# Edge passes of a graph attention kernel in another layout: groups of ten with a carry column, 79 tiles, one addition over 1024 columns, the next weights split first, the join prepared in the drain

## What is computed

```python
loops = arange(N); src, dst = concat([src, loops]), concat([dst, loops])
xl = (x @ Wl + bl).reshape(N, H, C)
xr = (x @ Wr + br).reshape(N, H, C)
e = leaky_relu(xl[src] + xr[dst], 0.2)
logits = einsum('ehc,hc->eh', e, att)
m = segment_max(logits, dst); p = exp(logits - m[dst])
alpha = p / segment_sum(p, dst)[dst]
out = segment_sum(xl[src] * alpha[..., None], dst) + bias
# x = x + layer1(elu(layer0(layernorm(x)))); x = x + ffn(layernorm(x))
```

## Time and profile before

| | |
|---|---|
| runs, median (range) | 3017.18 us (3014.49 to 3019.19) |
| profiled execution | 3014.56 us, its span 3012.7 us |
| busy in the span | PE 87%, DVE 83%, ACT 50%, POOL 41% |
| edge pass 0 / 1, first addition to the next stage's first DMA | 559.0 to 1043.5 us / 1597.2 to 2081.3 us |
| VectorE busy, 640 to 960 / 1680 to 2000 us | 308.15 / 310.85 of 320 us |
| tiles started in each of these | 58 / 58 |
| granted TensorE clock there | 0.95 / 0.94 |
| DMA share there | 0.86 / 0.86 |

### The profile page before, as it was taken

One profiled execution on the slowest core, in us unless ns is written; L12 is line 12 of the kernel. 1 busy time (PEld: TensorE's weight loads), 2 busy tenths in 40 slices (PEclk: granted clock), 3 DMA queues, 4 the chain that ended last, 5 costly groups with the idle time before them and its releaser, 6 DMA issues. The chain is left out here.

```text
span 3012.7 us, 40248 instructions
## 1 busy us (share of the span) xinstructions
PE 2627.5 (87%) x11205; PEld 1801.0 (60%) x11205; DVE 2505.0 (83%) x5771; ACT 1503.3 (50%) x3651; POOL 1236.6 (41%) x1138
## 2 busy tenths in 40 slices
PE   6999999788888099999989888861899999969997
PEld 5777777333333078888864333330788888746665
DVE  7999998699999467777757999994988888379997
ACT  4545555155555333333323555553777788525554
POOL 0012220577776133333317777752333333014443
PEclk8999999899999599999999999985899999989998
DMA  9999999588887588888856888876999999469999
GB/s 326 340 308 319 320 323 342 179 235 243 231 238 211 142 272 279 269 265 266 263 197 204 243 239 237 237 186 202 385 357 352 347 349 344 140 183 250 249 250 160
DMA packets 321178, 789.66 MB, mean 262 GB/s; under 512 B 53838, under 2 KB 54384, under 8 KB 310746
## 3 DMA queue, kind: packets, MB, share of 16 engines
q1 hardware_dynamic: 220440, 540.20, 51.2%
q0 software_dynamic: 98064, 243.10, 33.3%
q10 hardware_dynamic: 2452, 3.79, 0.4%
HBM read 469.66 MB, written 329.28 MB: 265 GB/s over the span
## 5 line engine op out<-in xcount | busy, mean ns | idle before, releaser
L882 PE MATMUL bank<-wr,nT_e 128*128 128x512 f32 x1280 | 610.6, 622 | 0.5 <-DVE z_e L735 0.5
L1039 PE MATMUL bank<-whi,t_hi 128*128 128x512 f32 x1256 | 524.0, 417 | 23.7 <-DVE t_lo L406 23.7
L1041 PE MATMUL bank<-whi,t_lo 128*128 128x512 f32 x1256 | 498.1, 397 | 0.0
L1040 PE MATMUL bank<-wlo,t_hi 128*128 128x512 f32 x1256 | 497.7, 396 | 0.0
L882 PEld LDWEIGHTS bank<-wr,nT_e 128*128 128x128 f32 x1280 | 244.3, 201 | 253.1 <-issue 252.4
L906 POOL DMA_INDIRECT vin<-touched,node_slot x157 | 173.5, 1105 | 333.2 <-DMA vin<-rows 329.8
L906 POOL DMA_INDIRECT g_vin<-touched,node_slot x157 | 176.9, 1127 | 323.2 <-DMA g_xin<-in_x 289.8
L676 ACT COPY nT_e<-bank 128x512 f32<-128x512 f32 x160 | 93.6, 585 | 409.3 <-PE bank L885 354.9
L1039 PEld LDWEIGHTS bank<-whi,t_hi 128*128 128x128 f32 x1256 | 237.2, 189 | 73.7 <-issue 17.2
L1041 PEld LDWEIGHTS bank<-whi,t_lo 128*128 128x128 f32 x1256 | 237.2, 189 | 58.8
L655 POOL TENSOR_TENSOR z_e<-z_e,v_att 128x512 f32<-128x512 f32 x160 | 204.8, 1280 | 158.6 <-DVE z_e L740 157.8
(11 more groups left out here) (247 smaller groups left out, 6001.5 us busy)
## 6 DMA issues: line engine op xcount, KB each, us to landing
rows<-t_row SPq DMA_DIRECT2D x312, 512.0 KB, 4.4
w_e<-w_e POOLq DMA_DIRECT2D x80, 512.0 KB, 4.7
touched<-acc_e SPq DMA_DIRECT2D x160, 256.0 KB, 4.3
xin<-in_x SPq DMA_DIRECT2D x156, 256.0 KB, 4.7
xTin<-in_xT SPq DMA_DIRECT2D x156, 256.0 KB
vin<-rows SPq DMA_DIRECT2D x156, 256.0 KB, 4.0
g_vin<-rows SPq DMA_DIRECT2D x156, 256.0 KB
g_xin<-in_x SPq DMA_DIRECT2D x156, 256.0 KB
```

The costliest lines, as they stand in the source:

```text
L882: pe.matmul(psR[b][:, :], nT[:, b, cc, :], wr[:, cc, :], start=(cc == 0), stop=False)
L1039: pe.matmul(ps, hi[:, cc, :], whi[:, cc, :], start=(cc == 0), stop=False)
L1040: pe.matmul(ps, hi[:, cc, :], wlo[:, cc, :], start=False, stop=False)
L1041: last = pe.matmul(ps, lo[:, cc, :], whi[:, cc, :], start=False, stop=(cc == KC - 1))
```

## The change

- G is 10 instead of 5, and the last groups are of five and four tiles (`LAST`, `group_sizes`): nine groups for T = 79 tiles.
- The logits, maxima and sums of a group lie in one row with a carry column in front of each head's columns (`lg`, `top`, `total`; width H x (n + 1)). What comes over from the group before stands in the carry column, so that the factor needs no instructions of its own; `same_w` and `gap_w` replace `same4`, `gap4` and `gap4_back`.
- `vs` and `nv` become one `ring` of R = 18 places with three rows of 512; `pair_sums` is one addition over 1024 columns, xr broadcast. GpSimd now multiplies the first half of `z`, VectorE the second.
- GpSimd gathers LEAD = 6 ahead instead of 7. Weighing follows `weigh_at`: 11 steps behind in groups of ten, and for the last 30 tiles (`CATCH`) two tiles a step once their group is ready; adding follows one step and accumulating three steps behind it.
- The split of the next weights stands at the start of a pass. `raw`, `brow`, `others`, `share`, `weigh_s`, `share_T` and `picked` lie in places of `w1`, `w2`, `z` and `nT`.
- The trailing values are stored as soon as the last shares are there; `picked` and the arithmetic of the join stand ahead of the last accumulations.
- Every Block has `no_gpsimd_drain=True`.

The core of the diff:

```diff
-G = 5
-R = 14
+G = 10
+LAST = (5, 4)
+CATCH = 30
+LEAD = 6
+R = 18
+OWN, SRC = 0, 1
...
-    with nc.Block() as block:
+    with nc.Block(no_gpsimd_drain=True) as block:
...
-    T = -(-(e_tiles) // G) * G
+    T = e_tiles
+    W = T + len(group_sizes(T))
...
+    weigh_at = []
+    for t in range(T):
+        i = group_of[t]
+        ready = first[i] + sizes[i] + 1
+        weigh_at.append(max(ready, weigh_at[-1] + (0 if t % 2 and t > T - CATCH else 1)) if t else ready)
+    steps = weigh_at[-1] + 5
+
+    def due(k, at, late):
+        return [t for t in range(T) if at[t] + late == k]
...
+            for t in range(T):
+                if t == late[0]:
+                    sp.wait_ge(s["trail_set"], 2)
+                    sp.dma_start(trails[:, :], trail[:, :, :].rearrange("p a h -> p (a h)")).then_inc(s["trail_stored"], 16)
+                if t == late[1]:
+                    sp.wait_ge(s["trail_stored"], 16)
+                    sp.dma_start(others.rearrange("p q a h -> p (q a h)"),
+                                 bcast(trails[:, :].rearrange("q a -> (q a)"))).then_inc(s["others_loaded"], 16)
+                store(t)
...
-            pipeline(T + G + 2, [(lambda t: product_own(t) if t < T else None, 1),
-                                 (lambda t: add_own(t - G - 2) if t > G + 1 else None, 0),
-                                 (lambda t: gather(t) if t < T else None, 7)])
+            for k in range(-LEAD, steps):
+                if 0 <= k + 1 < T:
+                    product_own(k + 1)
+                for t in due(k, weigh_at, 1):
+                    add_own(t)
+                if 0 <= k + LEAD < T:
+                    gather(k + LEAD)
...
+            act.wait_ge(s["w_loaded"], 16)
+            act.copy(whi[:, :, :], raw).then_inc(s["w_high"], 1)
...
+            for k in range(-4, steps):
+                if 0 <= k + 4 < T:
+                    copy_transposed(k + 4)
+                for t in due(k, weigh_at, 0):
+                    weigh(t)
+                if 0 <= k < T:
+                    exps(k)
...
-                dve.tensor_tensor(z[:, b, 0, :], psR[t % 2][:, :], vs[:, u, :], ALU.add)
-                dve.tensor_tensor(z[:, b, 1, :], psR[t % 2][:, :], nv[:, u, 1, :], ALU.add).then_inc(s["z"], 1)
+                dve.tensor_tensor(z[:, b, :, :], psR[t % 2][:, :].unsqueeze(1).to_broadcast([P, 2, D]), ring[:, u, 1:3, :],
+                                  ALU.add).then_inc(s["z"], 1)
...
+                if i:
+                    dve.tensor_scalar(l[:, SRC, :, 0], columns(top, i - 1)[:, :, sizes[i - 1]], gap[:, at:at + 1], None, ALU.add)
+                link(dve.tensor_tensor(l[:, OWN, :, 1:], l[:, OWN, :, 1:], start_gap[:, at:at + n].unsqueeze(1).to_broadcast([P, H, n]),
                                        ALU.add))
+                link(dve.tensor_tensor(m, lg[:, OWN, a:b], lg[:, SRC, a:b], ALU.max))
+                link(dve.tensor_tensor_scan(m, gap_w[:, a:b], m, -BIG, ALU.add, ALU.max))
+                link(dve.tensor_tensor_scan(back(top, a, b), back(gap_w, a + 1, b + 1), m[:, ::-1], -BIG, ALU.add, ALU.max))
+                dve.tensor_tensor(lg[:, :, a:b], lg[:, :, a:b], top[:, a:b].unsqueeze(1).to_broadcast([P, 2, b - a]),
+                                  ALU.subtract).then_inc(s["bottom"], 1)
...
+                    link(dve.tensor_tensor(carry, carry, columns(total, i - 1)[:, :, sizes[i - 1]], ALU.mult))
+                link(dve.tensor_tensor(q, lg[:, OWN, a:b], lg[:, SRC, a:b], ALU.add))
+                link(dve.tensor_tensor_scan(total[:, a:b], same_w[:, a:b], q, 0.0, ALU.mult, ALU.add))
+                link(dve.tensor_tensor_scan(v[:, ::-1], back(gap_w, a + 1, b + 1), back(total, a, b), -BIG, ALU.add, ALU.max))
+                link(dve.reciprocal(v, v))
+                dve.tensor_tensor(lg[:, :, a:b], lg[:, :, a:b], v.unsqueeze(1).to_broadcast([P, 2, b - a]),
+                                  ALU.mult).then_inc(s["shares"], 1)
...
+            for k in range(-3, T):
+                for step, ahead in ((leaky, 2), (logits, 1), (pair_sums, 3), (product, 2), (peaks, 1)):
+                    if 0 <= k + ahead < T:
+                        step(k + ahead)
+                for t in due(k, weigh_at, 3):
+                    accumulate(t)
+                if k >= 0:
+                    sums_up(k)
+                if k == T - 1:
+                    dve.wait_ge(s["shares"], NC)
+                    dve.tensor_copy(trail[:, 0, :], columns(top, NC - 1)[:, :, sizes[-1]]).then_inc(s["trail_set"], 1)
+                    dve.tensor_copy(trail[:, 1, :], columns(total, NC - 1)[:, :, sizes[-1]]).then_inc(s["trail_set"], 1)
...
+def group_sizes(T):
+
+    sizes = []
+    while sum(sizes) < T - sum(LAST):
+        sizes.append(min(G, T - sum(LAST) - sum(sizes)))
+    return sizes + list(LAST)
```

More of the change, by code:

```diff
@@ L33 @@
 DR = 5
-SR = 4
 MR = 8
@@ L569, in edge_pass, with span, columns, columns2 @@
     places = touched[:, :].rearrange("(p t) d -> p t d", p=P)
-    N, NC = g["N"], T // G
     following = "Wl1" if layer == 0 else "gfc1T"
+    sizes = group_sizes(T)
+    first = [sum(sizes[:i]) for i in range(len(sizes))]
+    group_of = [i for i, n in enumerate(sizes) for _ in range(n)]
+    NC, W = len(sizes), T + len(sizes)
+    top_size = max(sizes)
+    def span(i):
+        a = H * (first[i] + i)
+        return a, a + H * (sizes[i] + 1)
+    def columns(buf, i):
+        a, b = span(i)
+        return heads(buf[:, a:b])
+    def columns2(buf, i):
+        a, b = span(i)
+        return buf[:, :, a:b].rearrange("p a (h n) -> p a h n", h=H)
+    def back(buf, a, b):
+        return buf[:, a:b][:, ::-1]
+    def share_of(buf, side, t, h):
+        i = group_of[t]
+        q = span(i)[0] + h * (sizes[i] + 1) + 1 + t - first[i]
+        return buf[:, side, q:q + 1]
+    def is_last(t):
+        return t == T - 1 or group_of[t + 1] != group_of[t]
+    weigh_at = []
+    for t in range(T):
+        i = group_of[t]
+        ready = first[i] + sizes[i] + 1
[3 more added lines that the diff above has]
+        return [t for t in range(T) if at[t] + late == k]
     with ExitStack() as c:
@@ L610, in edge_pass @@
             g["gathered_before"][t % R] += 32
-        block = c.enter_context(nc.Block())
+        block = c.enter_context(nc.Block(no_gpsimd_drain=True))
+        late = [t for t in range(T) if weigh_at[t] + 3 >= T]
         @block.sync
@@ L752, in logits @@
                                   ALU.add).then_inc(s["logit"], 1)
             def peaks(t):
-                i, last = divmod(t, G)
-                if last != G - 1:
+                if not is_last(t):
                     return
-                b, at = i % 2, i * G
-                l, m, e = lg[:, b, :, :, :], peak[:, b, :, :], ex[:, b, :]
-                factor = e[:, 2 * H * G:]
+                i = group_of[t]
+                at, n = first[i], sizes[i]
+                a, b = span(i)
@@ new lines, in _ @@
+            for i, n in enumerate(sizes):
+                dve.tensor_copy(picked[:, 0, :, first[i]:first[i] + n], columns(top, i)[:, :, 1:])
+                last = dve.tensor_copy(picked[:, 1, :, first[i]:first[i] + n], columns(total, i)[:, :, 1:])
+            link(last)
+            link(dve.tensor_tensor(picked.rearrange("p a h t -> p (a h) t"), picked.rearrange("p a h t -> p (a h) t"),
+                                   first_end[:, :].unsqueeze(1).to_broadcast([P, 2 * H, T]), ALU.mult))
@@ L839, in _ @@
+            link(dve.tensor_reduce(picked2[:, :, :], picked, AX.X, ALU.add))
+            mine = picked2
+            for k in range(T, steps - 2):
+                for t in due(k, weigh_at, 3):
+                    accumulate(t)
             dve.wait_ge(s["others_loaded"], 16)
[L840 removed]
+            link(dve.tensor_tensor(share, others[:, :, 0, :].rearrange("p q h -> p h q"),
                                    g["joins"][:, :].unsqueeze(1).to_broadcast([P, H, P]), ALU.add))
[L842 removed]
+            link(dve.tensor_reduce(best[:, :], share, AX.X, ALU.max))
```

202 lines of the change are left out of this document (73 added, 129 removed).

## The result

The changed kernel takes 3168.97 us (median of four, 3163.68 to 3178.37) against 3017.87 (3014.49 to 3019.19) beside it: ratio 1.0506, interval 1.0475 to 1.0537. It is slower, as forecast, but by 151 us instead of 20, outside the range. The profiled execution took 3174.08, its span 3172.4, where the forecast's sum had 3034.6. Medians are of all executions of a kernel; the one exception is e12, where an execution of 4848.36 us at a granted clock of 0.75 instead of 0.94 is left out.

What follows compares the result with a forecast made beforehand. VectorE bound the kernel at 5.40 us a tile, gather waits just under it. Two passes at +16 (start and steady part) and -4 (tail), and -4.2 for the last drain, gave +20: 3037 us (3034.6 profiled), range 2990 to 3075.

Steps and rivals of the forecast that it cites:

- tail: From a pass's last addition to the next stage: 55.5 us instead of 59.4, -4 us a pass.
- the price of the round: Chain of leaky, gather, transposes, root product and addition advances three tiles instead of four: 17.2 us, 5.73 a tile.
- issue to transposes: From GpSimd's issue of the second gather to TensorE's transposes: 5.74 us, or 5.16 on a lighter load.
- transposes to the addition: From TensorE's transposes through the root product to VectorE's addition: 4.63 us at the high clock.
- addition to leaky: On VectorE, from the addition to the next leaky: 2.40 us, with the 0.06 saved taken off.
- the merging: On VectorE, two additions over 512 columns become one over 1024: 0.06 us a tile saved.
- the drains: no_gpsimd_drain removes GpSimd's drain, 4.6 us at each edge pass's end and 4.2 at the kernel's end.
- the weight split: At the start of a pass: costs nothing, or up to 2 us if weights land after the first transposes.
- a shorter round: Rival, chance 0.20: the round is shorter than rows with waits say, 5.5 us a tile, 2995 us.
- a lead that does not matter: Rival, chance 0.08: VectorE's work alone counts, 5.1 us a tile from the twentieth on, 2931 us.
- The loss of the high clock: Rival, chance 0.12: TensorE's root products at half clock in half of the tiles, +0.3 us a tile, 3075 us.
- the longer tail: Rival, chance 0.11: last group's weighings stand ahead of its exponentials and the drain's wait turns up elsewhere, 3055 us.

Runs made afterwards that it cites:

- e12: e4 with the catch-up only for the last 12 tiles (CATCH = 12 instead of 30): 2958.06 us, ratio 0.9801.
- e1: The kernel before with one edit, GpSimd gathering 6 ahead instead of 7: 3160.93 us, ratio 1.0475.
- e2: The changed kernel with TensorE's transposes 5 ahead instead of 6, so a round advances four tiles: 2989.12 us, ratio 0.9906.
- e7: The changed kernel with LEAD = 7 instead of 6, groups of ten and 18 ring places kept: 3002.6 us, ratio 0.9956.
- e14: The changed kernel with one unused matmul of 128 columns behind every bias product of TensorE: 3147.13 us, ratio 1.0416.
- e3: The changed kernel without the catch-up (CATCH = 0 instead of 30): 3114.7 us, ratio 1.0322.
- e4: The changed kernel with groups of eight instead of ten and gathers 8 ahead instead of 6: 2967.41 us, ratio 0.9834.
- e9: e4 without the catch-up (CATCH = 0): 2955.09 us, ratio 0.9789.
- e6: The kernel before with no_gpsimd_drain=True in every Block and nothing else: 3002.4 us, ratio 0.9953.
- e8: e4 with the one addition over 1024 columns taken apart into two over 512: 2974.26 us, ratio 0.9858.

## Why the forecast was wrong

By its own steps, for pass 0 (pass 1 in brackets), against 3034.6 for the profiled execution:

| stretch | forecast | measured | off |
|---|---|---|---|
| first addition to tile 20 | 104.5 | 108.7 (101.0) | +4 (-4) |
| tiles 20 to 60 | 40 x 5.8 = 232 | 259.4 (261.2) | +27 (+29) |
| tiles 60 to 78 | 18 x 5.8 = 104 | 140.4 (135.2) | +36 (+31) |
| tail | 55.5 | 61.2 (61.8) | +6 (+6) |

In all +74 and +63, 137 of the 139.5 us that are off; the rest lies outside the passes, 2 of it at the end of the kernel.

**The step that failed is the price of the round**, 17.2 us for three tiles. The mechanism and the round were right (e1, e2, e7). Its four legs, as means over tiles 20 to 60 of the first pass:

| leg | forecast | measured |
|---|---|---|
| leaky to the second gather's issue | 4.68 | 4.92 |
| issue to transposes | 5.45 | 6.12 |
| transposes to the addition | 4.63 | 5.69 |
| addition to leaky | 2.40 | 2.73 |
| round | 17.2 | 19.5 |

- Issue to transposes: the gather itself was no later, since it lands after 5.1 us on the mean. But the transposes start only 1.1 us behind the landing, because they stand behind another tile's root product; the rows had shown only tiles for which TensorE waited.
- Transposes to the addition, the largest: 0.66 us of it is the mean root product, 4.26 instead of 3.60. The forecast had the high clock in this leg and left the low one to a rival, since it spread the pauses evenly at 1.3 us a tile. They bunch: three tiles then meet one pause of 3 to 5.5 us, the root product behind it runs in part at the low clock (14 of 41 do), and the same round pays for it.
- Addition to leaky: the group work, which was counted as a delay of 1.1 us in ten tiles.

Together 19.5, 6.5 a tile. With the clock mostly back (e14) the round takes 18.6: of 2.3 us, about 0.9 is the clock (1.0 in the second pass, 19.3 to 18.2), and the rest the queue and the group work. This split rests on the one profiled execution of e14.

**The second failed step is an omission**: 5.8 a tile was carried to the last tile, though the change has ScalarE weigh two tiles a step in the last 30. ScalarE then waits for accumulations, GpSimd for weighings, and the gathers behind them are later than this lead covers. Under LEAD = 6 that is 22 to 25 us a pass before the last addition (e3); the remaining 9 to 12 us of this stretch are the round's price. With gathers 8 ahead the catch-up still costs 12 us there (e4 against e9).

**The tail** was forecast 4 us shorter and is 2 us longer. The last shares come at +21.8 (forecast +20.5); four weighings behind them take 12.0 us instead of 9.4, 2.3 of it ScalarE's wait for an accumulation; the rest up to the next stage takes 27.4 instead of 25.6. The drain went as forecast: from the scatter to the next stage pass 5.5 us (1124.73 to 1130.22) instead of the 10.1 before (1033.44 to 1043.53), and e6 agrees.

**What held:** the merging (0.06; e8 0.05), the drains (-13.4; e6 -14.4), that the weight split costs nothing that shows (first addition 560.48; 560.37 and 559.97 in e1 and e6, which have no split at the start), VectorE's pace when fed (4.67 a tile without group work). With group work a fed VectorE needs 5.2 (e2, e4) and not the 5.1 of the forecast; in 5 of the 40 tiles its product there takes 1.88 us beside GpSimd's. Of the rivals, a shorter round and a lead that does not matter fell with e1. The loss of the high clock happened, but with tiles at 6.5 instead of 6.1, and the longer tail happened for other reasons than the one named. The page "DMA: Bandwidth & Descriptors" of the Trainium skill (latency and other measured facts), by which a lighter load on HBM makes the fixed cost of a transfer smaller, was given as support for the shorter round. The source's gather, the second of a tile, does not agree: its median landing is 5.0 us here at a DMA share of 0.72 and 4.8 in e2 at 0.86. The target's does, 4.9 against 5.4, and the transposes came later nevertheless.

## What to carry to other kernels

A step taken out of a lead makes a round advance one tile less: count how many tiles are left, and price it with the queue in front of each engine and with the group work in it, not only with the rows of tiles that waited. Rounds that ran interleaved moved together here, so count their waits as one long one and price TensorE's work behind it by rows at the lower clock; here the clock took about 0.9 of the round's 2.3 us of excess. A catch-up of one engine is paid where other engines' orders wait for it: try it with zero before fine sizes, and put arithmetic that is early enough behind the instruction for which a store waits.

## What was not expected of the hardware

With unused matmuls of 128 columns behind each root product the granted clock was 0.92 instead of 0.87 and the kernel 22 us of 3169 faster; with 512 columns it was 0.97 and 18 us. VectorE's product over 512 columns takes 1.88 us where GpSimd's product of the same shape starts with it, and 0.68 otherwise (e4, e9); the addition over 1024 columns with one operand in PSUM takes 1.21 us either way.
